# Side units of an attention phase cut into quarters and put behind the first chunk of each step

## The reference

```python
Q = split_heads(x @ Wq.T + bq); K = split_heads(x @ Wk.T + bk); V = split_heads(x @ Wv.T + bv)   # x is normalised first
scores = einsum("bhqd,bhkd->bhqk", Q, K) / sqrt(hd) + prior_lambda * gaussian_mask
out = einsum("bhqk,bhkd->bhqd", softmax(scores), V) @ Wo.T + bo
```

## Time and profile before

| | |
|---|---|
| time, median of 3 runs | 5565.44 us (5561.8 to 5568.02) |
| the profiled execution | 5561.3 us, span 5559.5 us |
| granted TensorE clock, mean over the span | 0.991 |
| busy share of the span: PE, DVE, ACT, POOL | 93%, 85%, 77%, 39% |
| the attention phase | about the first 2940 us of the span |

### The profile page before, as it was taken

One profiled execution on the slowest core, in us unless ns is written; L12 is line 12 of the kernel. 1 busy time (PEld: TensorE's weight loads), 2 busy tenths in 40 slices (PEclk: granted clock), 3 DMA queues, 4 the chain that ended last, 5 costly groups with the idle time before them and its releaser, 6 DMA issues. The chain is left out here.

```text
span 5559.5 us, 179608 instructions
## 1 busy us (share of the span) xinstructions
PE 5193.5 (93%) x75212; PEld 3169.5 (57%) x75340; DVE 4744.1 (85%) x9925; ACT 4269.2 (77%) x8522; POOL 2185.2 (39%) x1695
## 2 busy tenths in 40 slices
PE   8889989999899998998888999999999999999999
PEld 2333333333333333333336888888887888888887
DVE  5998899998999889999967888887776888888776
ACT  3999999999999999999994777776334777777333
POOL 2011103211032110220006998995113999897222
PEclk8999999999999999999999999999999999999999
DMA  2011101111011111111103454543001454454211
GB/s 86 23 34 38 38 24 45 42 44 40 25 38 48 38 40 29 50 42 36 30 12 93 113 117 111 117 113 98 12 10 43 114 117 113 112 118 106 60 52 46
DMA packets 262970, 343.32 MB, mean 62 GB/s; under 512 B 45664, under 2 KB 165520, under 8 KB 262160
## 3 DMA queue, kind: packets, MB, share of 16 engines
q1 hardware_dynamic: 262160, 331.84, 24.0%
HBM read 104.14 MB, written 33.55 MB: 25 GB/s over the span
## 5 line engine op out<-in xcount | busy, mean ns | idle before, releaser
L659 ACT ACTIVATE a_pr<-a_w,a_expscale 128x512 f32<-128x512 f32 x4096 | 2455.6, 698 | 59.6 <-PE a_w L543 33.7
L811 DVE TENSOR_REDUCE a_mx<-a_b 128x1 f32<-128x512 f32 x2688 | 1705.3, 683 | 124.1 <-PE a_b L528 117.3
L528 PE MATMUL a_b<-a_kp,a_qp 48*32 48x512 f16 x16384 | 1424.1, 383 | 197.8 <-DVE a_mx L809 92.4
L543 PE MATMUL a_w<-a_qp,a_kp 50*32 50x512 f16 x16384 | 1459.4, 383 | 51.7 <-ACT raw L642 39.0
L565 PE MATMUL a_po<-a_pr,a_v 64*17 64x512 f32 x16384 | 1165.1, 591 | 21.5 <-ACT a_osb L692 20.6
L528 PEld LDWEIGHTS a_b<-a_kp,a_qp 48*32 48x32 f16 x16384 | 403.2, 90 | 1272.4 <-DVE a_mx L811 627.0
L809 DVE CUSTOM_DVE_ANT_0 a_junk<-a_b,a_gw 128x512 bf16<-128x512 f32 x1408 | 962.9, 684 | 105.2 <-PE a_b L528 50.1
L1709 POOL TENSOR_TENSOR l_p<-l_p,l_rc 128x512 f32<-128x512 f32 (+1 forms) x512 | 721.8, 1437 | 31.3 <-DVE l_rc L1607 31.1
L1497 ACT ACTIVATE l_p<-l_S,l_nm 128x256 f32<-128x256 f32 (+1 forms) x1024 | 470.9, 470 | 203.6 <-DVE l_nm L1599 203.6
L1351 PE MATMUL l_G<-l_wqkv,l_hT 128*128 128x512 f32 x2304 | 603.0, 406 | 9.4 <-DVE l_hT L1550 8.2
L543 PEld LDWEIGHTS a_w<-a_qp,a_kp 50*32 50x32 f16 x16384 | 413.8, 90 | 284.5 <-ACT a_pr L659 117.7
(11 more groups left out here) (258 smaller groups left out, 8855.6 us busy)
## 6 DMA issues: line engine op xcount, KB each, us to landing
l_qs<-l_qT SPq DMA_DIRECT2D x512, 128.0 KB, 2.3
l_kh<-l_kT SPq DMA_DIRECT2D x512, 128.0 KB, 2.4
l_kl<-l_kT SPq DMA_DIRECT2D x256, 128.0 KB, 2.4
a_qp<-q_parts SPq DMA_DIRECT2D x128, 128.0 KB, 2.8
a_kp<-k_parts SPq DMA_DIRECT2D x128, 128.0 KB, 3.1
l_tab<-in_rotary SPq DMA_DIRECT2D x128, 128.0 KB, 2.4
a_xc<-in_x SPq DMA_DIRECT2D x28, 512.0 KB, 3.9
q_parts<-raw SPq DMA_DIRECT2D x32, 256.0 KB, 2.3
```

The lines of the kernel that those rows point to most:

```text
L528: m = eng.matmul(bk[32 * r:32 * r + 32, :], qp[s][0:DEEP, o:o + 32], kp[s][0:DEEP, c * 512:c * 512 + 512], start=True, stop=True)
L543: m = eng.matmul(bk[32 * r:32 * r + 32, :], kp[s][HALF:HALF + DEEP + 2, o:o + 32], qp[s][HALF:HALF + DEEP + 2, c * 512:c * 512 + 512], sta ...
L659: eng.activation(pr[(2 * n + c // 2) % NP][:, o:o + 512], banks[i], ACT.Exp, scale=expscale[:, :]).then_inc(s_free[i], 1)
L811: t = eng.tensor_reduce(mx[g % 2][:, qb, c:c + 1], banks[i], X, ALU.max)
```

## The change

Each `project`, `values` and `out_project` of the main loop becomes four pieces of 128 columns of its bank, each `spread` two pieces of 256, and each piece gets a step of its own, in successive steps (`in_pieces`). A piece takes a bank of the ring by itself. All units, and `rows_T`, move from behind the fourth chunk of their step to behind its first chunk, on PE and on ACT. ACT reads each piece with one instruction. For a `project` in pieces ACT writes only the float32 part, and POOL makes both fp16 parts when the last piece has been read: a copy of 128x512 and then the subtraction. `turned` stays whole, and so do the units of the start and those behind the loop. `moments` moves to steps 19, 27, ... of a batch (18, 26, ... before), `inverses` to step 6 (5 before), `stats` to steps 102, 137 and 172 (105, 142 and 175 before; the first stays at 75).

```diff
+PIECES = dict(project=4, values=4, spread=2, out_project=4)
...
+    def in_pieces(n, what):
+        for k in range(PIECES[what[0]]):
+            n = plan(n, *what, k) + 1
+        return n
...
         if b:
-            side[plan(n0 + 5, "project", b, 1, 3, "k")] = ("inverses", b - 1)
+            in_pieces(n0 + 2, ("project", b, 1, 3, "k"))
+            beside(n0 + 6, "inverses", b - 1)
             for w0 in range(0, W, 2):
-                plan(n0 + 8 + 4 * w0, "spread", b - 1, w0)
-                plan(n0 + 10 + 4 * w0, "out_project", b - 1, w0)
-                side[n0 + 18 + 4 * w0] = ("moments", b - 1, w0)
+                in_pieces(n0 + 9 + 4 * w0, ("spread", b - 1, w0))
+                in_pieces(n0 + 13 + 4 * w0, ("out_project", b - 1, w0))
+                beside(n0 + (83 if w0 == W - 2 and b + 1 < NB else 19 + 4 * w0), "moments", b - 1, w0)
...
-                    if what[:4] != ("project", b + 1, 1, 3) or (what[4] == "q" and b + 1 == NB - 1):
-                        while what[0] == "project" and n % W in (11, 12, 13):
-                            n += 1
-                        n = plan(n, *what) + (5 if what[0] == "project" else 3)
+                    if what[0] == "turned":
+                        n = plan(n, *what) + 3
+                    elif what[:4] != ("project", b + 1, 1, 3) or (what[4] == "q" and b + 1 == NB - 1):
+                        if k == 6 and j < 3:
+                            beside(n, "stats", b + 1, j + 1)
+                        n = in_pieces(n, what) + (what[0] == "project")
...
@@ def attention_tables
-        if n in units:
-            unit(units[n], COLUMNS)
+            if c == 0 and n in units:
+                unit(units[n], COLUMNS)
+            if c == 0 and rows_at(n):
+                t.take(("rows", rows_at(n) - 1), COLUMNS)
...
@@ def tensor (the same on ACT)
             for c in range(4):
                 pass1(n, c)
                 pass2(n, c)
+                if c == 0 and n in units:
+                    work[units[n][0]](units[n])
+                if c == 0 and rows_at(n):
+                    rows_T(("rows", rows_at(n) - 1))
                 if c == 2:
                     pv(n - 1)
-            if n in units:
-                work[units[n][0]](units[n])
-            if rows_at(n):
-                rows_T(("rows", rows_at(n) - 1))
...
@@ def scalar, project
+            if part is not None:
+                o = 128 * part
+                eng.activation(tmp[(m - 1) % 4][:, o:o + 128], banks[i][:, o:o + 128], ACT.Identity, **scaled).then_inc(s_free[i], 1)
+                return
...
@@ def gpsimd, project_lo
+            if what in slot:
+                pool.wait_ge(s_whole, m)
+            else:
+                pool.wait_ge(*stored(m - 4))
+                eng.tensor_copy(z[:, 0, :], tmp[(m - 1) % 4][:, :]).then_inc(s_hi, 1)
+                pool.wait_ge(s_hi, m - WHOLE)
             eng.tensor_tensor(z[:, 1, :], tmp[(m - 1) % 4][:, :], z[:, 0, :], ALU.subtract).then_inc(s_lo, 1)
```

More of the change, by code:

```diff
@@ L168, in first_units, with whole, piece, ends @@
     return out
+PIECES = dict(project=4, values=4, spread=2, out_project=4)
+FULL = dict(turned=4, project=5, values=4, spread=3, out_project=3)
+def whole(what):
+    return what[:FULL[what[0]]]
+def piece(what):
+    return what[-1] if len(what) > FULL[what[0]] else None
+def ends(what):
+    return piece(what) in (None, PIECES.get(what[0], 0) - 1)
 EARLY_VALUES = [("values", 0, j, half) for j in range(3) for half in range(2)]
@@ L260, in unit @@
         nonlocal n_hT
-        used[what] = len(count["ob"])
-        if what[0] in ("spread", "out_project") and what[1] < NB - 1:
-            tick("ob", what)
+        base = whole(what)
+        used.setdefault(base, len(count["ob"]))
+        if ends(what) and what[0] in ("spread", "out_project") and what[1] < NB - 1:
+            tick("ob", base)
         if what[0] == "turned" and what[3] == 0:
@@ L478, in values @@
             pe.wait_ge(s_const, CONST)
-            for i in range(2):
+            for i, n0, n in spans(what):
                 o = (2 * half + i) * 128
@@ L492, in spread @@
             pe.wait_ge(s_rp, 5 * (b + 1))
-            for c in range(2):
+            for c in range(2) if piece(what) is None else (piece(what),):
                 for k in range(3):
@@ L622, in values @@
         def values(what):
-            _, b, j, half = what
+            _, b, j, half = whole(what)
             i, k = slot[what]
@@ L682, in scalar @@
                 pass2(n, c)
[L683 to L686, removed]
+                if c == 0 and n in units and units[n][0] in work:
+                    work[units[n][0]](units[n])
+                if c == 0 and rows_at(n):
+                    rows_T(("rows", rows_at(n) - 1))
             if n > 0 and n % W == 0:
@@ L1040, in gpsimd @@
                     normal(units[n + 1])
-                if units[n + 1][0] == "spread" and units[n + 1][2] % 4 == 0:
+                if units[n + 1][0] == "spread" and units[n + 1][2] % 4 == 0 and piece(units[n + 1]) == 0:
                     biased(units[n + 1][1], units[n + 1][2] // 4)
             if n in units:
-                after = units[n] if units[n][0] in ("project", "spread", "out_project") else None
+                after = whole(units[n]) if units[n][0] in ("project", "spread", "out_project") and ends(units[n]) else None
         head_sum(NB * HA - 1)
@@ L1183, in sync @@
                 second(side[n - 2])
-            if n - 2 in units and units[n - 2][0] == "out_project":
-                store(units[n - 2])
+            if n - 2 in units and units[n - 2][0] == "out_project" and ends(units[n - 2]):
+                store(whole(units[n - 2]))
             if after:
@@ L1191, in sync @@
                     turned(units[n])
-                after = units[n] if units[n][0] == "project" else None
+                after = whole(units[n]) if units[n][0] == "project" and ends(units[n]) else None
             if rows_at(n):
```

86 lines of the change are left out of this document (49 added, 37 removed).

## The result

The changed kernel takes 5652.26 us (median of 4 runs, 5643.72 to 5673.56) against 5565.5 us: a ratio of 1.0162, 95% interval 1.0134 to 1.0191. It is slower by 87 us; the forecast was +66, 5632 us, in a range of 5550 to 5690.

What follows compares the result with a forecast made beforehand. In plain steps DVE was taken as the limit, with side units costing 205 us; pieces 204 - 205, DVE's side work +29, waits +23 and +22, and -7 gave +66, 5632 us, range 5550 to 5690.

Steps and rivals of the forecast that it cites:

- The step of 2.87 us: Steps with a piece: the third score tile waits for the bank of the step's first, 0.47 us over plain 2.40.
- (a): Rival: bank order does not bind; piece steps take what ACT needs, 2.61 or 2.43 us; 5485 us, chance 0.17.
- (d): Rival: ACT becomes the bound by a fixed cost of each read; piece step 2.71 us, total 5572, chance 0.04.
- (b): Rival: bank order binds, but waits and bursts do not add, as ACT and DVE have stored work; 5575, chance 0.14.
- (c): Rival: worse; PE waits drain both rings, each piece costs 0.51 us, waits at upper bounds; 5691, chance 0.09.
- The division itself gains nothing: Main loop: pieces and whole turned cost 204 us in all, where the old side units cost 205.
- 46 us or more on average: Sign in the profile after: length of heads in the project stretch, as before the change.
- DVE's side work, +29: stats, moments and reciprocals on DVE, mostly hidden before by steps where DVE ran dry, now cost 29 us.
- the -7: Credit of 7 us: in heads where PE waits for rows, the DVE burst of moments falls into that wait.
- ACT waits for `ob`, 1.9 each: At spread right after a finished head, ACT waits for POOL's head_sum and out_project: 12 times, 23 us.
- PE waits for `rows`, 2.2 each, ten times: At rows_T (n % 16 == 13) after moments, PE waits for POOL while DVE and ACT run dry: 22 us.
- 45.5 to 46.5: Sign in the profile after: average length in us of heads in the out_project stretch.

Runs made afterwards that it cites:

- e9_half_the_sums: e6_no_waits with each project, values and out_project piece summing half its products, spread a third; that computation left out: 5566.52 us.
- e10_row_ring: e6_no_waits with the main loop's units taking banks from the row-tile ring that DVE reads, instead of the column ring: 5620.44 us.
- e2_rows_last: The changed kernel with rows_T alone moved back behind the fourth chunk: 5614.35 us, ratio 1.0082.
- e8_pool_parts_alone: The kernel before, units whole and in their old places, but ACT reads each project once and POOL makes both fp16 parts: 5537.36 us.
- e4_moments_20: The changed kernel with moments one step later, at steps 20, 28, ...: 5604.93 us, ratio 1.0066.
- e6_no_waits: The changed kernel with spread one step later and moments at steps 20, 28, ...: 5567.41 us, ratio 0.9998.

## Why the prediction was right

- **The step of 2.87 us** (2.84 to 2.91): right, and its cause is shown. Most steps with a piece measure 2.84 to 2.93 us, whatever the piece is (medians 2.88 to 2.91, and 2.85 in the step in which ACT also empties `po`); half of PE's work taken away changes nothing (e9_half_the_sums); the same order in the other ring makes the same step (e10_row_ring). PE's weight loads waited for ACT 270.6 us, forecast over 200. Rivals (a) and (d) are out, and so is (b), since undoing the two waits gave time back; the bounds of (c) were not reached. `rows_T` is one more such tile, which the prediction did not count: the 28 steps that have it and no piece take 2.91 us too (2.66 in e2_rows_last).
- **"The division itself gains nothing"**: right. 409.0 for 412.5 us in the nine heads, and 5567.4 against 5565.5 us without the waits. Two things cancel there: POOL making both parts gains 28 us (e8_pool_parts_alone), which pieces behind the first chunk give back. The sign "46 us or more on average" for those heads was missed by little: 45.4.
- **DVE's side work, +29, and the -7**: right for `moments`, wrong for the -7. In the changed kernel the 22 plain steps behind a `moments` cost 18 us (e4_moments_20), where I had 17 for 24. They cost it before a wait for `rows` as well: the window of 3.22 us above is such a step, so the -7 did not come. What is left, pieces and the other side work with all else that moved, came to +2 us (e6_no_waits), where the terms (204 - 205 + 10 + 2) give +11. That a `moments` can be free is seen in that run: a head with 12 piece steps and two `moments` took 45.50 us, and 40.4 + 12 x 0.47 alone is 46.0.
- **ACT waits for `ob`, 1.9 each**: right. That step takes 5.69 us, where others with a piece at n % 16 == 1 take 3.76: 1.93, so 23 us. It came 12 times, as forecast.
- **PE waits for `rows`, 2.2 each, ten times**: right. PE stands 2.0 to 2.6 us, ten times. Where the granted clock stayed at 1.00, the step took 5.05 us, 1.8 more than the 3.25 of the same step in e6_no_waits, so 18 us. Eight of the ten took 6.40 to 6.64 us, and these have the lower clock in them:

```profile
911.27:916.32 5.05, 2.97 (x77) 1.29 (x77) 3.19 (x8) 2.96 (x7) 2.77 (x5) 1.00 0.26 76
1651.58:1658.22 6.64, 4.54 (x77) 1.56 (x77) 3.23 (x8) 2.96 (x6) 2.79 (x5) 0.63 0.25 80
```

- **What was missing: the clock.** The two waits and the place of `moments` are 23 + 18 + 18 = 59 us, but undoing them gave back 5652.3 - 5567.4 = 85. Two windows of the kernel after, in and behind one wait for `ob`:

```profile
874.50:877.60 3.10, 1.28 (x24) 0.38 (x24) 1.61 (x4) 1.01 (x3) 2.50 (x2) 1.00 0.03 8
877.60:886.00 8.40, 7.37 (x152) 2.57 (x160) 5.35 (x12) 7.40 (x15) 1.28 (x1) 0.80 0.38 111
```

  In the wait PE is busy 1.28 of 3.10 us, at full clock. Behind it the granted clock is 0.80 over 8.4 us: 3.4 of them are at the 1.2 GHz level. PE there, and ACT behind it:

```profile
880.15 0.64 PE L582 MATMUL a_w<-a_qp,a_kp 50*32 50x512 f16 x4
...
880.57 1.67 PE L604 MATMUL a_po<-a_pr,a_v 64*17 64x512 f32 x16
...
882.56 1.84 ACT L711 ACTIVATE a_pr<-a_w,a_expscale 128x512 f32<-128x512 f32 x3 [0.83 <-PE a_w L582]
```

  A group of scores takes 0.64 us for 0.40 and `pv` 1.67 for 1.08, ACT idles 0.83 us more, and that step takes 3.82 us. The same kernel shows what it takes at full clock, for of the 12 waits for `ob` one, at 2363 us, was not followed by the lower level. The step behind it, and the same step one head later:

```profile
2366.73:2369.59 2.86, 2.64 (x70) 1.27 (x70) 1.66 (x5) 2.71 (x6) 1.23 (x1) 1.00 0.33 86
2420.14:2424.27 4.13, 3.91 (x68) 1.59 (x68) 1.86 (x5) 2.71 (x6) 1.27 (x1) 0.63 0.30 75
```

  The other 11 take 3.82 to 4.32 us, 13.5 more in sum. The eight slow waits for `rows` take 12 more than at full clock, and the steps behind them 2: 28 us in this execution. The loops of the two profiled executions differ by 89 us up to the last head, and 59 + 28 is 87 of them. By the trace's clock records this stretch has 106 us at the lower level, and 14 in e6_no_waits, so that a microsecond there costs 0.3, an estimate. That the waits bring the clock down is shown by its return when they go. For the medians, 85 - 59 leaves 26 us to the clock.

  The profiled execution is 21 us over the median, for the most part for another reason: from 2984.4 us on, in the last head, where PE makes no row tiles any more, the clock was at the lower level to the loop's end, and the last 20 steps took 64.8 us, where they take 48.1 in e6_no_waits.

```profile
2984.40:3034.40 50.00, 49.82 (x504) 13.69 (x504) 0.00 (x0) 33.26 (x56) 0.00 (x0) 0.50 0.02 4
```

  Without that stretch its mean clock would be 0.983, as in the other three executions, of which there are no traces. No wait for `ob` or `rows` stands before it, and what brought the clock down there stays open.

The sum: +2 for pieces and the other side work where I had +11, +18 for `moments` where I had +17 less 7, +41 for the waits where I had +45, and +26 for the clock where I had nothing. The mechanisms named were the right ones, but that the total came so near is partly luck: the clock was missing, and terms of 9 and 4 us too high stood against it. One forecast contradicted its own sum: "45.5 to 46.5" for heads with `out_project`. The terms give 40.4 + 12 x 0.47 + 1.4 + 1.9 + 2.2 = 51.5, and 52 to 54.5 us were measured. The waits for L471 on ACT went, as forecast. The rule of the Trainium skill ("ScalarE: Activation LUTs", "Rules for kernel authors"), by which a 128-column read would be an estimate of 0.41 us, lies between what the trace shows for the two kinds, by form in the groups of ACT:

```profile
L672 ACT ACTIVATE a_v<-a_w 128x128 f32<-128x128 f32 x96 | 26.7, 278 | 0.0
...
L689 ACT ACTIVATE a_tmp<-a_w,a_sbq,a_unit_of 128x128 f32<-128x128 f32 x48 | 22.1, 460 | 0.0
```

The project piece takes 0.46, where I had 0.43. The next exponential starts 0.16 us behind such a copy of 0.28 (at 357.36, behind the one at 357.20 above), so 0.12 us of it is covered.

## What to carry to other kernels

Before cutting work into small pieces that share a ring of buffers, write down for each tile which earlier tile must be read first, the inserted piece's own buffer included, and add up the loop from "buffer freed" to "freed again". Here that number gave the step in every placement (2.87 and 3.26 us, and by the rows 2.65, which no run separates from another reading), and the size of a piece hardly entered. Then look at what the new steps bring together (one shared buffer, one in-order engine that two others wait for): two such meetings and the side work of DVE beside them cost 85 us here, 26 of them through the clock, and moving `spread` and `moments` by one step removed them. And undo a change's parts separately, for they may pull apart: one read less on ACT was worth 28 us by itself, and with the pieces behind the last chunk and no new waits the whole came to 5499 us, 1.2% under the kernel before.

## What had not been expected of the hardware

Waits of some 2 us of TensorE in an otherwise full loop (idle 1.8 of 3.1 us at `ob`, 2.0 to 2.6 at `rows`) are followed by stretches at the 1.2 GHz level, behind 11 of 12 and 8 of 10 of them. In the changed kernel, 106 us of the loop up to the last head are at that level, in 22 stretches, 19 of them in or behind one of the two waits. With one kind of wait removed it is 61 and 58 us, with both removed 14, and 3.4 us in the kernel before. Over the nine heads above, PE was busy 386.2 of 409.0 us, with waits of 0.43 and 0.45 us in a step with a piece, and the clock was 0.99. A microsecond at the lower level cost about 0.3 us of the loop (28 us for 92 more), by the working above.
